# Attention on one core: partial sums in four consecutive groups, each merged when complete, and the output banks evacuated by VectorE

## The reference

```python
def attn(x, Wq, Wk, Wv):                    # 16 heads of 32
    q, k, v = (heads(x @ W.T) for W in (Wq, Wk, Wv))
    energy = einsum('nhqd,nhkd->nhqk', q, k)
    return merge_heads(einsum('nhql,nhld->nhqd', softmax(energy / sqrt(32), axis=3), v))
def ffn(x, weights, scale, bias):
    w = (weights >= 0) * 2.0 - 1.0
    return clip(einsum('bsi,oi->bso', x, w) * scale + bias, -100, 100)
x = layernorm(x + attn(x, Wq, Wk, Wv))
x = layernorm(x + ffn(x, weights, scale, bias))
```

## Time and profile before

| | |
|---|---|
| Median of three runs | 3019.92 us |
| The profiled execution, its own time | 3020.84 us |
| Its span, first to last instruction | 3019.0 us |
| Mean granted TensorE clock | 0.981 of full speed |
| Busy over the span | TensorE 94%, ScalarE 78%, VectorE 73%, GpSimd 11% |
| `attend`, from the first to the last instruction of its loops | about 606 to 2734 us |

### The profile page before, as it was taken

One profiled execution on the slowest core, in us unless ns is written; L12 is line 12 of the kernel. 1 busy time (PEld: TensorE's weight loads), 2 busy tenths in 40 slices (PEclk: granted clock), 3 DMA queues, 4 the chain that ended last, 5 costly groups with the idle time before them and its releaser, 6 DMA issues.

```text
span 3019.0 us, 78291 instructions
## 1 busy us (share of the span) xinstructions
PE 2832.8 (94%) x29292; PEld 1429.3 (47%) x29292; DVE 2197.3 (73%) x1922; ACT 2344.3 (78%) x2902; POOL 343.1 (11%) x340
## 2 busy tenths in 40 slices
PE   8999999899999999999989999899999999997998
PEld 7888888633333333333333333333333333335887
DVE  4433334378878787788778778777877877786998
ACT  3333333399989889898989999898998989894665
POOL 0000000010000000000000000000000000003665
PEclk9999999999999999999999999999999999998999
DMA  5454454447566655756566575656657565654563
GB/s 199 167 186 176 167 183 178 169 108 158 114 147 136 146 134 129 156 114 147 129 143 136 124 167 114 143 122 152 139 124 154 118 152 112 153 113 142 204 207 126
DMA packets 223344, 444.15 MB, mean 147 GB/s; under 512 B 15410, under 2 KB 130098, under 8 KB 198836
## 3 DMA queue, kind: packets, MB, share of 16 engines
q0 software_dynamic: 27216, 198.19, 32.8%
q1 hardware_dynamic: 186596, 224.71, 23.3%
q10 hardware_dynamic: 9216, 16.78, 1.5%
HBM read 123.47 MB, written 117.96 MB: 80 GB/s over the span
## 4 chain that ended last, share of the span: by engine, by line
PE 40%; DMA 14%; issue 11%; ACT 8%; DVE 7%; POOL 1%; ACTq 0%; DVEq 0%; POOLq 0%; SPq 0%
PE banks L633 15%; PE banks L662 15%; DMA sums<-sums 14%; ACT probs L770 7%; PE banks L998 6%; DVE sums L821 6%; PE banks L678 2%; PE banks L987 1%; PE banks L980 1%; DVE sums L817 1%; PE banks L994 0%; ACT wf_scaled L750 0%; POOL sums L601 0%; POOL score_rows L583 0%; PE banks L981 0%
## 5 line engine op out<-in xcount | busy, mean ns | idle before, releaser
L770 ACT ACTIVATE probs<-banks 128x1024 f32<-128x1024 f32 x2048 | 1908.0, 1172 | 91.0 <-PE banks L633 81.5
L633 PE MATMUL banks<-score_rows 97*32 97x512 f16 x16384 | 1227.6, 385 | 70.2 <-ACT probs L770 29.2
L662 PE MATMUL banks<-probs,v_keys 128*32 128x512 f32 x8192 | 1162.6, 597 | 16.8 <-issue 15.4
L821 DVE TENSOR_TENSOR sums<-sums,probs 128x2048 f32<-128x2048 f32 x512 | 1134.4, 2282 | 23.9 <-ACT probs L770 23.7
L633 PEld LDWEIGHTS banks<-score_rows 97*32 97x32 f16 x16384 | 438.7, 96 | 1043.5 <-ACT probs L770 572.9
L817 DVE TENSOR_TENSOR sums<-probs 128x2048 f32<-128x2048 f32 x256 | 569.4, 2286 | 396.7 <-ACT probs L770 396.7
L662 PEld LDWEIGHTS banks<-probs,v_keys 128*32 128x32 f32 x8192 | 295.2, 112 | 241.4 <-issue 64.2
L345 DVE TENSOR_TENSOR qk_lo<-banks,qk_hi 128x512 f16<-128x512 f32 x128 | 88.5, 691 | 239.3 <-ACT qk_hi L289 239.3
L289 ACT ACTIVATE qk_hi<-banks 128x512 f16<-128x512 f32 x128 | 76.4, 597 | 232.6 <-PE banks L243 232.6
L243 PE MATMUL banks<-xT_hi,w_hi 128*128 128x512 f32 x512 | 201.2, 393 | 1.5 <-DVE xT_lo L321 1.5
L243 PE MATMUL banks<-xT_hi,w_lo 128*128 128x512 f32 x512 | 199.3, 389 | 0.0
(11 more groups left out here) (92 smaller groups left out, 2157.8 us busy)
## 6 DMA issues: line engine op xcount, KB each, us to landing
sums<-sums POOLq DMA_DIRECT2D x189, 1024.0 KB, 8.5
x_in<-in_L_attn_x SPq DMA_DIRECT2D x17, 1024.0 KB, 7.1
scratch_q_raw<-qk_raw SPq DMA_DIRECT2D x16, 1024.0 KB, 5.5
scratch_k_raw<-qk_raw SPq DMA_DIRECT2D x16, 1024.0 KB, 5.6
scratch_v<-v_out SPq DMA_DIRECT2D x16, 1024.0 KB, 5.0
score_rows<-scratch_q_hi SPq DMA_DIRECT2D x128, 128.0 KB, 3.0
score_rows<-scratch_k_hi SPq DMA_DIRECT2D x128, 128.0 KB, 2.9
v_keys<-scratch_v SPq DMA_DIRECT2D x64, 256.0 KB, 6.5
```

Source lines behind the costliest of these rows:

```text
L633: last = nc.tensor.matmul(scores_of(unit)[part, i, :], k_rows[:, h, keys], q_rows[:, h, qb * BLK:(qb + 1) * BLK], start=True, stop=True)
L662: last = nc.tensor.matmul(banks[rows, out_bank(qb), :], v_keys[:, kt, rows], probs[:, kt % P_RING, h, :], start=(kt == 0), stop=(kt == KT ...
L770: nc.scalar.activation(probs[:, kt % P_RING, heads, :], scores_of(qb * UNITS + u), ACT.Exp, scale=SCALE / GAIN ** 2).then_inc(a_prob, 1)
L821: nc.vector.tensor_tensor(total, total, probs[:, kt % P_RING], ALU.add).then_inc(a_sum, 1)
```

## The change

In `attend` the four interleaved chains become four consecutive groups of four key tiles (`PER` = 4). Group 0 is summed into `total`, groups 1 to 3 into `partial`, each by three additions, the first of which adds two tiles of the ring. In groups 1 to 3 GpSimd adds the group's partial sum to `total` by an accumulating DMA as soon as the group is complete, one at a time, three per block as before. In the last block the last group isn't merged, and TensorE sums `total` and that group by 16 matmuls. An addition now waits for the one just before it. Both copies of the output bank move from ScalarE to VectorE: the numerators behind the addition of tile 2, the denominators behind that of tile 13. TensorE's denominators move from tile 12 to tile 10 of the next block. VectorE's first item is peeled off its loop. At the end of `project` SyncE waits for the last block's stores also.

```diff
--- before.py
+++ after.py
@@ -48,11 +48,14 @@
 BOUND_SQ_MAX = (BOUND_MAX / SCALE) ** 2 * GAIN ** 4
 BOUND_SLACK = 1.04
 NORM_SQ_MAX = 60000.0 ** 2 / BOUND_SLACK
-CHAINS = 4
+GROUPS = 4
+PER = KT // GROUPS
 P_RING = 8
 SLOTS = 3
 LAG = 2
-DEN_TILE = 12
+DEN_TILE = 10
+OUT_AFTER = 2
+DEN_AFTER = 13
 
 
 def project(nc, ctx, dram, args, banks, ffn):
@@ -157,9 +160,9 @@
             sp.wait_ge(s_hi, b * NP + NP + 4)
             sp.dma_start(dram["v"][bass.ds(b, 1)].rearrange("o (t p) d -> p (o t) d", p=P),
                          v_out[:]).then_inc(s_vst, 16)
-        sp.wait_ge(s_qst, 48 * NBLK)
-        sp.wait_ge(s_kst, 48 * NBLK)
-        sp.wait_ge(s_vst, 16 * NBLK)
+        sp.wait_ge(s_qst, 48 * NBLK + 48)
+        sp.wait_ge(s_kst, 48 * NBLK + 48)
+        sp.wait_ge(s_vst, 16 * NBLK + 16)
         sp.wait_ge(s_x, 16 * (NBLK + 1))
 
     @block.gpsimd
@@ -390,7 +393,8 @@
     k_exact = rows32[0:HD + 1, 1]
     v_keys = sb("v_keys", [P, KT, P], FP32)
     probs = sb("probs", [P, P_RING, G, BLK], FP32)
-    sums = sb("sums", [P, 2, CHAINS, G, BLK], FP32)
+    total = sb("total", [P, 2, G, BLK], FP32)
+    partial = sb("partial", [P, GROUPS - 1, G, BLK], FP32)
     ones = sb("ones", [P, HD], FP32)
 
     q_head = probs[0:HD, 0].rearrange("p h t -> p (h t)")
@@ -413,8 +417,8 @@
     a_pv = sem("a_pv")
     a_sum = sem("a_sum")
     a_order = sem("a_order")
-    a_half = sem("a_half")
     a_merge = sem("a_merge")
+    a_merged = sem("a_merged")
     a_den = sem("a_den")
     a_out = sem("a_out")
     a_dout = sem("a_dout")
@@ -593,28 +597,28 @@
         pool.sem_inc(m_store, 16)
         pool.sem_inc(m_neg, 1)
 
-        def merge(it, qb):
+        def merge(it, qb, groups):
 
             st = it * QB + qb
-            pool.wait_ge(a_sum, (st + 1) * KT + P_RING)
-            pool.sem_inc(a_order, 1)
-            pool.dma_start(sums[:, qb % 2, 0], sums[:, qb % 2, 1], accum_op=ALU.add).then_inc(a_half, 16)
-            pool.dma_start(sums[:, qb % 2, 2], sums[:, qb % 2, 3], accum_op=ALU.add).then_inc(a_half, 16)
-            pool.wait_ge(a_half, st * 32 + 32)
-            pool.sem_inc(a_order, 1)
-            pool.dma_start(sums[:, qb % 2, 0], sums[:, qb % 2, 2], accum_op=ALU.add).then_inc(a_merge, 16)
+            for g in groups:
+                pool.wait_ge(a_sum, st * KT + PER * (g + 1) + P_RING)
+                pool.sem_inc(a_order, 1)
+                pool.dma_start(total[:, qb % 2], partial[:, g - 1], accum_op=ALU.add).then_inc(a_merge, 16)
+                pool.wait_ge(a_merge, (st * (GROUPS - 1) + g) * 16)
+                pool.sem_inc(a_merged, 1)
 
         with pool.Fori(0, LAST) as it:
             for qb in range(QB):
-                merge(it, qb)
-        for qb in range(QB - 1):
-            merge(LAST, qb)
+                merge(it, qb, range(1, GROUPS))
+        for qb in range(QB):
+            merge(LAST, qb, range(1, GROUPS if qb < QB - 1 else GROUPS - 1))
 
 
     @block.tensor
     def _(pe):
         pe.sem_inc(a_pv, P_RING)
         pe.sem_inc(a_den, 2)
+        pe.sem_inc(a_merged, GROUPS - 1)
 
         def fast_scores(it, qb, kt):
             if kt == 0:
@@ -665,18 +669,19 @@
 
         def denominators(it, qb):
             st = it * QB + qb
+            parts = [total[:, qb % 2]]
             if it is LAST and qb == QB - 1:
+                pe.wait_ge(a_merged, (st + 2) * (GROUPS - 1) - 1)
                 pe.wait_ge(a_sum, (st + 1) * KT + P_RING)
-                chains = CHAINS
+                parts.append(partial[:, GROUPS - 2])
             else:
-                pe.wait_ge(a_merge, st * 16 + 16)
-                chains = 1
+                pe.wait_ge(a_merged, (st + 2) * (GROUPS - 1))
             pe.wait_ge(a_out, st + 1)
-            for chain in range(chains):
+            for part in parts:
                 for h in range(G):
                     rows = slice(HD * h, HD * h + HD)
-                    last = nc.tensor.matmul(banks[rows, out_bank(qb), :], ones[:], sums[:, qb % 2, chain, h, :],
-                                            start=(chain == 0), stop=(chain == chains - 1))
+                    last = nc.tensor.matmul(banks[rows, out_bank(qb), :], ones[:], part[:, h, :],
+                                            start=(part is parts[0]), stop=(part is parts[-1]))
             last.then_inc(a_den, 1)
 
         def steps(scores, it, qb, tiles):
@@ -743,18 +748,7 @@
 
         nc.scalar.activation(wf_hi[:], wf_scaled[:], ACT.Copy).then_inc(a_wfhi, 1)
 
-        def copy_out(st, parity):
-            act.wait_ge(a_wflo, 1)
-            act.wait_ge(a_pv, st * KT + KT + P_RING)
-            act.wait_ge(a_store[parity], (st - parity) * 16 + 32)
-            nc.scalar.activation(out_sb[:, parity, :], banks[:, out_bank(parity), :], ACT.Copy).then_inc(a_out, 1)
-
-        def copy_den(st, parity):
-            act.wait_ge(a_den, st + 1 + 2)
-            act.wait_ge(a_store[parity], (st - parity) * 16 + 32)
-            nc.scalar.activation(den_sb[:, parity, :], banks[:, out_bank(parity), :], ACT.Copy).then_inc(a_dout, 1)
-
-        def item(it, first):
+        def item(it):
             for qb in range(QB):
                 st = it * QB + qb
                 for u in range(UNITS):
@@ -769,16 +763,9 @@
                     heads = slice(2 * half, 2 * half + 2)
                     nc.scalar.activation(probs[:, kt % P_RING, heads, :], scores_of(qb * UNITS + u), ACT.Exp,
                                          scale=SCALE / GAIN ** 2).then_inc(a_prob, 1)
-                    if u == 2 * LAG - 1 and not (first and qb == 0):
-                        copy_out(st - 1, (qb - 1) % 2)
-                    if u == 2 * (LAG + DEN_TILE) + 1 and not (first and qb == 0):
-                        copy_den(st - 1, (qb - 1) % 2)
-
-        item(0, True)
-        with act.Fori(1, ITEMS) as it:
-            item(it, False)
-        copy_out(ITEMS * QB - 1, 1)
-        copy_den(ITEMS * QB - 1, 1)
+
+        with act.Fori(0, ITEMS) as it:
+            item(it)
 
     @block.vector
     def _(dve):
@@ -803,22 +790,45 @@
                 dve.wait_ge(m_store, h * 16 + 16)
                 nc.vector.tensor_scalar(max_neg[:], banks[0:KT, 0, 0:P], -1.0, None, ALU.mult).then_inc(m_neg, 1)
 
-        with dve.Fori(0, ITEMS) as it:
+        def copy_out(st, parity):
+            dve.wait_ge(a_wflo, 1)
+            dve.wait_ge(a_pv, st * KT + KT + P_RING)
+            dve.wait_ge(a_store[parity], (st - parity) * 16 + 32)
+            nc.vector.tensor_copy(out_sb[:, parity, :], banks[:, out_bank(parity), :]).then_inc(a_out, 1)
+
+        def copy_den(st, parity):
+            dve.wait_ge(a_den, st + 1 + 2)
+            dve.wait_ge(a_store[parity], (st - parity) * 16 + 32)
+            nc.vector.tensor_copy(den_sb[:, parity, :], banks[:, out_bank(parity), :]).then_inc(a_dout, 1)
+
+        def item(it, first):
             for qb in range(QB):
                 st = it * QB + qb
-                for kt in range(CHAINS, KT):
-                    total = sums[:, qb % 2, kt % CHAINS]
+                for kt in range(KT):
+                    g, place = divmod(kt, PER)
+                    if place == 0:
+                        continue
+                    into = total[:, qb % 2] if g == 0 else partial[:, g - 1]
                     dve.wait_ge(a_prob, st * UNITS + 2 * kt + 2 + SLOTS)
-                    if kt < 2 * CHAINS:
-
-                        dve.wait_ge(a_den, st + 1)
-
-                        freed = 1 if kt < 2 * CHAINS - 1 else CHAINS + 1
-                        nc.vector.tensor_tensor(total, probs[:, kt - CHAINS], probs[:, kt], ALU.add).then_inc(a_sum, freed)
+                    if place == 1:
+                        if g == 0:
+                            dve.wait_ge(a_den, st + 1)
+                        else:
+                            dve.wait_ge(a_merged, st * (GROUPS - 1) + g)
+                        nc.vector.tensor_tensor(into, probs[:, (kt - 1) % P_RING], probs[:, kt % P_RING], ALU.add).then_inc(a_sum, 2)
                     else:
-
-                        dve.wait_ge(a_sum, st * KT + (kt - CHAINS + 1 if kt >= 3 * CHAINS - 1 else kt - 2 * CHAINS + 1) + P_RING)
-                        nc.vector.tensor_tensor(total, total, probs[:, kt % P_RING], ALU.add).then_inc(a_sum, 1)
+                        dve.wait_ge(a_sum, st * KT + kt + P_RING)
+                        nc.vector.tensor_tensor(into, into, probs[:, kt % P_RING], ALU.add).then_inc(a_sum, 1)
+                    if kt == OUT_AFTER and not (first and qb == 0):
+                        copy_out(st - 1, (qb - 1) % 2)
+                    if kt == DEN_AFTER and not (first and qb == 0):
+                        copy_den(st - 1, (qb - 1) % 2)
+
+        item(0, True)
+        with dve.Fori(1, ITEMS) as it:
+            item(it, False)
+        copy_out(ITEMS * QB - 1, 1)
+        copy_den(ITEMS * QB - 1, 1)
 
 
 def normalise_and_ffn(nc, ctx, dram, x, ffn, first, banks, out):
```

## The result

The changed kernel took 3055.31 us (median of 4 runs, 3054.51 to 3060.79) against 3019.23 us before (median of four): a ratio of 1.0124, with a 95% interval of 1.0106 to 1.0141. It is slower by 36 us, where I had forecast a gain of 161 us. The profiled execution has a span of 3053.8 us, and TensorE's mean granted clock fell from 0.981 to 0.960.

The account below looks back on a forecast made before the run. ScalarE was taken to pace the attention at 30.3 us a block, with 188 us of stops. Gains and losses summed to 162.3 us off the profiled 3020.8 us: 2858 us against the median, range 2825 to 2905 us.

Parts of the forecast that it names:

- The stops inside a matmul group: TensorE halting within 8 matmuls, 1.18 us at 1681.12, taken for instruction fetches held up by 2 MB of queued merges.
- VectorE's dependent additions: Additions waiting for the one before: 2.32 us each, VectorE 28.8 us a block; rival of VectorE as bound, 2897 us, 0.12.
- the chain of three: Three merges a block, one behind the other, 7.7 us each; rival that they set the pace, 3196 us, chance 0.04.
- my rivals: VectorE bound 2897 us (0.12), lockstep 2910 (0.11), no fetch stops 2839 (0.08), merge chain 3196 (0.04), wait stays 2960+ (0.03).
- TensorE's stop at the jump: ScalarE's stop when TensorE jumps to its loop top: 2.08 us an item, 28.1 us of the 91.0 us idle.
- the lost pause: ScalarE's copy pause softening the stop at the jump back; losing it was to cost 15 x 0.15, put at 3 us.
- The wait that I counted as a pure loss: ScalarE's denominator copy waiting for denominators that await a merge; its removal was to gain 71.1 us.
- "clock kind": ScalarE's stops, 1.81 us, behind a denominator wait, put down to TensorE's lowered clock; 24.5 us to be gained.
- The copies' 60.5 us: Gain from taking two copies a block off ScalarE: 0.96 us in each of 63 blocks.
- The third kind of stop: ScalarE's stops at three other places, 2.84 us in the item read, 38.4 us in all; half, 19.2 us, forecast as gained.
- the 162 us that I had summed: Total gain: 60.5 + 71.1 + 8.5 + 24.5 - 22 - 3 + 19.2 + 3.5 = 162.3 us.

Follow-up runs that it names:

- no_merges: Changed kernel with ScalarE's first item peeled off its loop and the merging DMAs left out, denominators still at tile 10: 2859.77 us, ratio 0.9475.
- act_peeled: Changed kernel with ScalarE's first item peeled off its loop again, so the function table load stands ahead of it: 3032.96 us, ratio 1.0058.
- groups_den7: Changed kernel with denominators at tile 7, ScalarE's first item peeled off and both copies still on ScalarE: 2948.24 us, ratio 0.9768.
- peeled_den7: Changed kernel with denominators at tile 7 and ScalarE's first item peeled off its loop: 2923.04 us, ratio 0.9683.
- peeled_den8: As peeled_den7, but with the denominators, and so TensorE's jump, at tile 8: 2918.69 us, ratio 0.9667.
- peeled_den9: As peeled_den7, but with the denominators, and so TensorE's jump, at tile 9: 2949.31 us, ratio 0.977.
- act_start16: As peeled_den7, with ScalarE's loop rotated so that its body begins at unit 16 of an item: 2940.73 us, ratio 0.9746.

## Why the prediction was wrong, point by point

*Right.* ScalarE paces at 0.917 us a unit. The block became 29.70 us. No denominator waits for a merge. The stops inside a matmul group were rightly put down to instruction fetches: in the kernel before each of TensorE's 35 stops of over 0.5 us for nothing shown, 14 of them at the jump, ends 1 to 2 us behind the end of an instruction packet. VectorE's dependent additions stand 2.33 us apart (2.32 said), and it still has gaps of 0.38 and 0.75 us in a block, so it isn't the bound. These are three of its rows:

```profile
1632.47 2.29 DVE L818 TENSOR_TENSOR partial<-probs 128x2048 f32<-128x2048 f32 x1
1634.80 4.62 DVE L821 TENSOR_TENSOR partial<-partial,probs 128x2048 f32<-128x2048 f32 x2
1639.79 2.29 DVE L818 TENSOR_TENSOR partial<-probs 128x2048 f32<-128x2048 f32 x1 [0.38 <-ACT probs L764]
```

A merge alone takes 7.0 to 10.0 us, median 8.0 (7.7 said), and the chain of three fits. So none of my rivals came true: the loss has a mechanism that I hadn't named.

*The step that failed: the stop at the jump, carried over unchanged.* I had TensorE's stop at the jump as its own kind (2.08 us an item) and added 0.15 us for the lost pause. But I moved the denominators, and so the jump, from behind a wait that ends when the last merge has landed, to 22.2 us of the block, when by my own times the first merge (18.3 to 26.0 us) is in flight. I also had the cause in hand: I took the stops inside a matmul group for fetches held up by merges. I didn't put it on the fetch of the jump. The wait that I counted as a pure loss was what kept the queues empty for it. At tile 10 the jump costs 5.79 + 1.48 + 0.42 us of ScalarE's time an item, not 2.2.

*The second: 24.5 us for the "clock kind".* The 1.81 us at 1664.07 I put down to the lowered clock behind the denominator wait. It stands at ScalarE's own jump, as a stop of 1.2 to 2.2 us does in each of 14 items. In the kernel before, the window 1660 to 1662 us has no packet, and 1662 to 1663 has these:

```profile
q1 hardware_dynamic: 157, 0.15, 48.0%
q14 instruction: 1, 0.01, 4.9%
```

The clock was in part at the lower level there (0.66 in the earlier trace rows), and may share in it, but in no_merges, where TensorE's stop is 2 us and ends long before, 1 us stays at this place. So I took a stop to vanish that was a jump's, and it grew to 5.5 us when the block's second merge came to be in flight there.

*The third: a line of the diff not costed.* ScalarE's loop isn't peeled any more, and the table load moved into it: 15 x 1.28 = 19 us, measured as 20 to 22 us by act_peeled. "ScalarE loses two copies" was all that I read from that part of the diff.

*Sizes.* The copies' 60.5 us are 0 alone, and 25 us once the denominator wait is gone: the rest hid TensorE's stops, for from groups_den7 to peeled_den7 ScalarE's idle time ahead of the exponentials rises by 35 us, from 96.5 to 131.1 us. The third kind of stop didn't go (1.95 us at 1681.70); over the middle 14 items it fell from 2.3 to 1.1 us an item, about the half that I had kept. A slip without weight: 15 x 0.15 us are 2 us and not the 3 us of my sum. The page of the Trainium skill that I cited (Runtime: NRT & Kernel Launch, "Instruction fetch mechanics") says that a taken branch outside the window waits for a fetch; this trace agrees, on two engines, with the numbers of the table. I used it for stops it calls hidden, and not for the jump that it warns of.

With both jumps less than 2 us behind a merge's issue (peeled_den8) the change gives 98 us (3016.85 - 2918.69); without any merges it would give 159 us (3018.33 - 2859.77). That this is close to the 162 us that I had summed is partly chance, since several terms of the sum were wrong.

## What to carry to other kernels

When a wait is removed or a piece of work is moved, look what else sits at that place: a loop's jump back asks for instructions, and here their packets came through only when a transfer of 1 MB was all but done. Put the jumps of long loops where no large transfer is in flight, and check it for each engine's loop. Read the diff for the loops too: ScalarE's function table was loaded in every iteration (16 loads) once the first one was no longer peeled off, and once in all when it was.

## What the runs showed of the hardware that I had not expected

- A 1 MB accumulating DMA holds up an instruction packet until it is nearly through, so that a jump costs about 5 to 7 us where it costs 0.9 to 3.4 us with no merge in flight (the table). Transfers by SyncE are held up likewise: in the window above, 6 of their packets ran beside 84 of the merge's, and 282 in the 1 us after it.
- It does so only from about 2.2 us after the merge is issued. Jumps up to 2.2 us behind an issue stopped ScalarE for mostly 1.1 to 1.8 us; between 2.3 and 2.4 us both 1.8 and 5.0 us occur. This fits the packets' times: a merge's first packets of data start 1.4 us behind its issue (the median of the changed kernel's 191), and ScalarE's instruction packet, where nothing holds it, starts up to 0.9 us ahead of the stop.
- For TensorE the edge lies between 1.7 and 2.3 us (stops of 2.9 and 5.5 us in peeled_den9), but below it the stops differ: 2.4 to 2.8 us at 0.6 to 1.1 us behind an issue (act_start16), and 3.5 to 4.2 us at 0.5 to 1.6 us behind (peeled_den8, with two packets and not one).
- Within a stretch without jumps or loads the kernel keeps its step to the hundredth: blocks of 29.70 and 29.69 us in a row, each with the same stop of 0.26 us.
